# Relation messages in a phase of their own, over edges ranked by relation, stored and gathered by edge

## What is computed

```python
def rgcn_layer(x, src, dst, edge_type, W, root, bias):
    xj = x[src]
    out0 = x @ root + bias
    def body(out, inputs):
        r, Wr = inputs
        mask = (edge_type == r).astype(x.dtype)
        s = segment_sum(xj * mask[:, None], dst, num_segments=N)
        cnt = segment_sum(mask, dst, num_segments=N)
        h = s / jnp.maximum(cnt, 1.0)[:, None]
        hb = h.reshape(N, 64, 4)
        return out + jnp.einsum('nbi,bio->nbo', hb, Wr).reshape(N, d), None
x = relu(rgcn_layer(x0, ..., W1, root1, bias1))
x = rgcn_layer(x, ..., W2, root2, bias2)
x1 = layernorm(x0 + x)
```

## Time and profile before

| | us |
|---|---|
| median of 3 runs | 9330.65 (9306.11 to 9335.38) |
| span of the profiled execution | 9339.1 |
| PE, DVE, ACT, POOL busy in it | 7917.3, 7634.8, 5028.6, 4377.3 |
| l1a, first to last gather's start | 2292.6 to 3490.9 |
| l1b, the same | 3506.0 to 4969.8 |

### The profile page before, as it was taken

The page is one execution under the profiler, slowest core; times in us unless marked ns, Lnnn a source line. Parts: engine busy times, 40 slices in busy tenths (PEclk is TensorE's granted clock), DMA queues, the critical chain, the costliest instruction groups (busy, mean ns, idle before and its releaser), DMA issues. The chain is left out here.

```text
span 9339.1 us, 213338 instructions
## 1 busy us (share of the span) xinstructions
PE 7917.3 (85%) x37713; PEld 5838.0 (63%) x37714; DVE 7634.8 (82%) x29986; ACT 5028.6 (54%) x17446; POOL 4377.3 (47%) x6104
## 2 busy tenths in 40 slices
PE   7661798888888887777778999989999999989999
PEld 2220777776666665555555666666666666668887
DVE  7665577777999889999997999887777767779998
ACT  0000088887223334444444777766666656667777
POOL 3771055554777765665653333332222222245554
PEclk7555599999999998999998999997666655589999
DMA  0002233333333334444443544443444434434444
GB/s 14 2 2 32 67 112 118 115 116 111 112 113 110 104 103 126 126 125 123 126 122 113 153 146 148 146 149 113 119 122 120 124 114 121 121 113 126 127 126 120
DMA packets 1075782, 1027.30 MB, mean 110 GB/s; under 512 B 201077, under 2 KB 1029893, under 8 KB 1074974
## 3 DMA queue, kind: packets, MB, share of 16 engines
q1 hardware_dynamic: 946910, 869.10, 30.6%
q0 software_dynamic: 128576, 155.65, 7.3%
HBM read 867.45 MB, written 318.18 MB: 127 GB/s over the span
## 5 line engine op out<-in xcount | busy, mean ns | idle before, releaser
L1077 PE MATMUL l1b_ps_b<-root,l1b_x_t 128*128 128x256 f32 x1584 | 485.6, 435 | 327.3 <-DVE l1b_message L990 327.2
L188 POOL DMA_INDIRECT l_gathered<-x,l_index x402 | 473.0, 1177 | 335.2 <-POOL l_index L184 184.2
L184 POOL COPY l2b_index<-by_src_meta 128x1 int32 (+1 forms) x406 | 84.2, 207 | 1135.4 <-PE l2b_ps_g L1558 1133.7
L1077 PEld LDWEIGHTS l1b_ps_b<-root,l1b_x_t 128*128 128x128 f32 x1584 | 327.0, 216 | 459.8 <-issue 410.7
L188 POOL DMA_INDIRECT l1a_gathered<-x,l1a_index x400 | 449.2, 1123 | 333.5 <-POOL l1a_index L184 315.1
L188 POOL DMA_INDIRECT l_gathered<-in_x,l_index x402 | 441.4, 1098 | 334.3 <-POOL l_index L184 183.7
L469 POOL DMA_INDIRECT item_records<-sort_slot_rec,sort_place x400 | 476.8, 1192 | 240.4 <-issue 232.8
L188 POOL DMA_INDIRECT l1b_gathered<-h,l1b_index x400 | 428.2, 1070 | 333.0 <-POOL l1b_index L184 300.0
L188 POOL DMA_INDIRECT l2b_gathered<-z,l2b_index x406 | 420.9, 1037 | 338.4 <-POOL l2b_index L184 204.4
L188 POOL DMA_INDIRECT l2a_gathered<-x,l2a_index x402 | 411.2, 1023 | 334.1 <-POOL l2a_index L184 243.6
L1077 PE MATMUL l1a_ps_b<-root,l1a_x_t 128*128 128x256 f32 x1584 | 422.1, 389 | 156.5 <-DVE l1a_message L990 156.5
(11 more groups left out here) (365 smaller groups left out, 26999.1 us busy)
## 6 DMA issues: line engine op xcount, KB each, us to landing
l2b_x<-z SPq DMA_DIRECT2D x414, 128.0 KB, 2.1
l2a_x<-x SPq DMA_DIRECT2D x410, 128.0 KB, 2.7
l1a_x<-x SPq DMA_DIRECT2D x406, 128.0 KB, 2.7
l1b_x<-h SPq DMA_DIRECT2D x406, 128.0 KB, 2.9
l1b_res<-x SPq DMA_DIRECT2D x404, 128.0 KB, 2.6
l2b_x_again<-z SPq DMA_DIRECT2D x404, 128.0 KB, 2.4
l_x<-in_x SPq DMA_DIRECT2D x402, 128.0 KB, 2.1
l_x<-x SPq DMA_DIRECT2D x402, 128.0 KB
```

What stands on the lines that cost most here:

```text
L184: pool.tensor_copy(index[:, slot, :], graph.meta[:, bass.ds(item, 1), OTHER].bitcast(I32))\
L188: pool.indirect_dma_start(gathered[:, slot, 0:D], None, source[0:N_NODES, :], bass.IndirectOffsetOnAxis(ap=index[:, slot, :], axis=0), bou ...
L1077: pe.matmul(sums, x_t[:, k, f * P:(f + 1) * P], root[:, f, :], start=(f == 0), stop=False)
```

## The change

Each edge gets a place in a list ordered by relation, where each relation begins at a full chunk of 128: 216 chunks. The ranking is done by DVE at the head of the sort, and the place travels as a fifth word of the edge's record. During `count_edges` POOL scatters the edges' sources to their places by 200 indirect DMAs. A new phase before each relation layer gathers the source rows of each chunk, transposes them, multiplies them with the relation's block weights laid out as two wide 128x128 matrices, and stores the messages. The relation layer then gathers messages instead of rows of x. The kind rows, the block product and DVE's two message steps go, and the bias add moves from POOL to DVE.

```diff
--- before.py
+++ after.py
-K3 = 3 * GROUP
+CHUNK_RING = 8
+CHUNKS = -(-(N_EDGES // P + R1) // CHUNK_RING) * CHUNK_RING
+MESSAGES = CHUNKS * P
...
-OTHER, NODE, KIND, WEIGHT = range(4)
+OTHER, NODE, KIND, WEIGHT, MESSAGE = range(5)
+FIELDS = 5
...
-def gather_rows(pool, graph, s, index, gathered, source, extra=0, more=None):
+def gather_rows(pool, graph, s, index, gathered, source, extra=0, field=OTHER, count=N_NODES):
...
-        pool.tensor_copy(index[:, slot, :], graph.meta[:, bass.ds(item, 1), OTHER].bitcast(I32))\
+        pool.tensor_copy(index[:, slot, :], graph.meta[:, bass.ds(item, 1), field].bitcast(I32))\
...
-        pool.indirect_dma_start(gathered[:, slot, 0:D], None, source[0:N_NODES, :],
+        pool.indirect_dma_start(gathered[:, slot, 0:D], None, source[0:count, :],
...
-            if more and k % 2:
-                step(Pair(g, k // 2 + ahead))
...
+                dve.memset(going_on[:], 1.0)
+                dve.tensor_copy(relations.source[:], raw[:, 0, :])
+                chain.step(dve.tensor_tensor(in_relation[:],
+                                             rec[:, 1, :, KIND].unsqueeze(1).broadcast_to([EP, R1, EC]),
+                                             c.iota[0:EP, 0:R1].unsqueeze(2).broadcast_to([EP, R1, EC]), ALU.is_equal))
+                chain.step(dve.memset(going_on[:, :, 0:1], 0.0))
+                chain.step(dve.tensor_tensor_scan(seen[:].rearrange("p r c -> p (r c)"),
+                                                  going_on[:].rearrange("p r c -> p (r c)"),
+                                                  in_relation[:].rearrange("p r c -> p (r c)"), 0.0, ALU.mult, ALU.add))
+                dve.tensor_copy(per_row[:], seen[:, :, EC - 1]).then_inc(s_per_row, 1)
+                dve.wait_ge(s_before_row, 1)
+                chain.step(dve.tensor_scalar(chunks_i[:], ps_rel[:, R1:2 * R1], float(P - 1), None, ALU.add))
+                chain.step(dve.tensor_single_scalar(chunks_i2[:], chunks_i[:], 7, op=ALU.logical_shift_right))
...
+                chain.step(dve.tensor_tensor(seen[:], seen[:], first_place[0:EP, :].unsqueeze(2).broadcast_to([EP, R1, EC]),
+                                             ALU.add))
+                chain.step(dve.tensor_tensor(seen[:], seen[:], in_relation[:], ALU.mult))
+                chain.step(dve.tensor_reduce(message[:], seen[:].rearrange("p r c -> p c r"), AX.X, ALU.add))
...
+                dve.scalar_tensor_tensor(relations.place[:], message_lane[:], float(CHUNKS), message_chunk[:],
+                                         ALU.mult, ALU.add)
+                chain.step(dve.tensor_tensor(passed_chunks[:],
+                                             last_chunk[0:1, :].unsqueeze(1).broadcast_to([1, CHUNKS, R1]),
+                                             c.iota[0:1, 0:CHUNKS].unsqueeze(2).broadcast_to([1, CHUNKS, R1]), ALU.is_le))
+                chain.step(dve.tensor_reduce(chunk_kind[:], passed_chunks[:], AX.X, ALU.add))
+                dve.tensor_scalar(relations.kind[:], chunk_kind[:], float(R1 - 1), None, ALU.min)
...
+                pool.memset(nobody[:], FAR).then_inc(s_nobody, 1)
+                pool.wait_ge(s_padded, 16)
+                for column in range(EC):
+                    part = column // LISTS
+                    if part >= 2 and column % LISTS == 0:
+                        pool.wait_ge(s_listed[part % 2], part // 2 * LISTS * 16)
+                    pool.indirect_dma_start(rel_source[:], bass.IndirectOffsetOnAxis(ap=relations.place[:, column:column + 1],
+                                                                                     axis=0),
+                                            relations.source[:, column:column + 1], None).then_inc(s_listed[part % 2], 16)
+                for k in range(2):
+                    pool.wait_ge(s_listed[k], EC // 2 * 16)
+                    pool.sem_inc(s_sources, 1)
...
+                sp.wait_ge(s_sources, 2)
+                sp.dma_start(relations.index[:], rel_source.rearrange("(p c) o -> p (c o)", p=P)).then_inc(s_indexed, 16)
+                sp.wait_ge(s_indexed, 16)
...
+                dve.tensor_scalar(graph.first[:], graph.keep[:], -1.0, 1.0, ALU.mult, ALU.add)
...
+def message_phase(nc, c, relations, name, blocks, x_in, messages):
...
+                sp.dma_start(wide[:], blocks).then_inc(s_wide, 16)
+                rows = messages.rearrange("(c p) d -> p c d", p=P)
+                with sp.Fori(0, laps) as lap:
+                    for n in range(R // 2):
+                        sp.wait_ge(s_message, lap * (R // 2) + (n + 1))
+                        sp.sem_inc(s_passed, 1)
+                        sp.dma_start(rows[:, bass.ds(lap * R + 2 * n, 2), :], message[:, 2 * n:2 * n + 2, :])\
+                            .then_inc(s_stored[n], 16)
...
+                pool.memset(gathered[:], 0.0).then_inc(s_zeroed, 1)
+                pool.wait_ge(s_zeroed, 1)
+                for chunk in range(CHUNKS):
+                    if chunk >= R:
+                        pool.wait_ge(s_turned, (chunk - R) // 2 + 1)
+                    pool.indirect_dma_start(gathered[:, chunk % R, :], None, x_in[0:N_NODES, :],
+                                            bass.IndirectOffsetOnAxis(ap=relations.index[:, chunk:chunk + 1], axis=0),
+                                            bounds_check=limit, oob_is_err=False).then_inc(s_g[chunk % R], 16)
...
+                def turn(lap, n):
+                    for k in (2 * n, 2 * n + 1):
+                        pe.wait_ge(s_g[k], (lap + 1) * 16)
+                        for f in range(2):
+                            last = pe.transpose(ps_x[n % 2][:, k % 2, f * P:(f + 1) * P], gathered[:, k, f * P:(f + 1) * P],
+                                                c.ident[:])
+                    last.then_inc(s_turned, 1)
+
+                def product(lap, n, kinds):
+                    pe.wait_ge(s_xt, lap * (R // 2) + (n + 1))
+                    for k in (2 * n, 2 * n + 1):
+                        for f in range(2):
+                            last = pe.matmul(ps_m[n % 2][:, k % 2, f * P:(f + 1) * P], x_t[:, k, f * P:(f + 1) * P],
+                                             wide[:, f, bass.ds(kinds[k], 1), :].rearrange("p r o -> p (r o)"),
+                                             start=True, stop=True)
+                    last.then_inc(s_product, 1)
...
+                with pe.Fori(0, laps - 1) as lap:
+                    pe.load(regs, relations.kind[0:1, bass.ds(lap * R, R)])
+                    kinds = [pe.snap(r, min_val=0, max_val=R1 - 1) for r in regs]
+                    for n in range(R // 2):
+                        if n < 2:
+                            pe.wait_ge(s_message, lap * (R // 2) + n)
+                        else:
+                            pe.wait_ge(s_message, lap * (R // 2) + (n - 1))
+                        product(lap, n, kinds)
+                        turn(lap + (n + 2) // (R // 2), (n + 2) % (R // 2))
...
+                with dve.Fori(1, laps) as lap:
+                    for n in range(R // 2):
...
+                        dve.wait_ge(s_product, lap * (R // 2) + (n + 1))
+                        dve.tensor_copy(message[:, 2 * n:2 * n + 2, :], ps_m[n % 2][:]).then_inc(s_message, 1)
...
-                move_tiles(sp, graph, s, x, x_in, result, x_out, later, lead=6)
+                move_tiles(sp, graph, s, x, x_in, result, x_out, later, lead=4)
...
-                gather_rows(pool, graph, s, index, gathered, x_in, more=(add_bias, 0 if residual is None else 2))
+                gather_rows(pool, graph, s, index, gathered, messages, field=MESSAGE, count=MESSAGES)
...
+                def add_bias(pair):
+                    if residual is None:
+                        dve.wait_ge(s["total"], pair.item + 3)
+                        dve.tensor_tensor(biased[:, pair.both, :], total[:, pair.both, :], both_bias, ALU.add)\
+                            .then_inc(s["biased"], 1)
+                    else:
+                        for j, k in pair.each():
+                            pass_wait(dve, s, s["in_res"][k], (pair.lap + 1) * 16)
+                        dve.tensor_tensor(biased[:, pair.both, :], res[:, pair.both, :], both_bias, ALU.add)\
+                            .then_inc(s["res_done"], 2)
...
-                steps = [(ready, 3), (lambda p: add_up(p, 0), 1), (lambda p: multiply(p, 0), 3), (lambda p: add_up(p, 1), 1),
-                         (lambda p: multiply(p, 1), 3)]
                 if residual is None:
-                    steps += [(make_hot, 3), (add_parts, 3), (make_kind, 6)]
+                    steps = [(lambda p: add_up(p, 0), 1), (make_hot, 3), (lambda p: add_up(p, 1), 1), (add_bias, 0)]
                 else:
-                    steps += [(add_residual, 1), (make_hot, 3), (add_parts, 3), (lambda p: norm.invert(dve, p), 0),
-                              (make_kind, 6), (lambda p: norm.shift(dve, p), 0), (centre, 1)]
```

(45 more changed lines are left out.)

219 lines of the change are left out of this document (120 added, 99 removed).

## The result

| | before | changed |
|---|---|---|
| median of the runs | 9333.0 us (9306.1 to 9384.8, 4 runs) | 8975.7 us (8903.2 to 9028.6, 4 runs) |
| profiled execution, its span | 9339.1 us | 8901.4 us |

The ratio is 0.961 (0.955 to 0.967). The forecast was 9177 with 8990 as its lower end: the change gained 357 us where 154 to 156 were forecast. The changed kernel was run again later, beside variants (e5): median 9007.2 (8811.5 to 9059.4, 6 runs) beside 9325.0, 0.966 by the medians. A ratio with an interval leaves out executions more than 1.5% above the quickest of their kernel, so that of e5, 0.950 (0.945 to 0.955), rests on two of its six, 8811.5 and 8913.0. The changed kernel spreads over 2.8% there, the kernel before over 0.7%. Runs e1 to e4, e5 to e8 and e9 to e12 were made at three times, each group on a chip of its own.

What follows compares the result with a forecast made beforehand. VectorE and GpSimd were taken to bound l1a, VectorE alone l1b. Terms -286 - 523 + 638 + 36 - 19 = -154 gave 9177 us against the median; 8-in-10 range 8990 to 9410.

Steps and rivals of the forecast that it cites:

- the signs named as right: l1a gathers 2.2 to 2.3 us apart, l1b's 2.3 to 2.4; 216 gathers in about 300 us; clock 0.9 or more.
- l1a: -286 forecast: First relation layer: GpSimd the next bound, an item falling from 2.96 to 2.25 us over 402 items.
- the case that each addition catches a copy: l1a: VectorE bias adds block GpSimd's index copies, 2.39 us an item rather than 2.25, 56 us more.
- l1b: -523 forecast: Second relation layer: an item falling from 3.65 to 2.35 us over 402 items, ends 2.12 and 2.85.
- The 0.15 us that I added: l1b: allowance per item above the largest of three bounds (2.05 to 2.2), which do not hide each other wholly.
- The rival of 2.85: l1b: loop of ScalarE and VectorE does not overlap, 2.85 us an item, gain 322 instead of 523, total 9378; chance 0.12.
- Message phases: +638 forecast: Two new phases before the relation layers: 216 chunks at 1.40 us plus 17 for phase change, 319 us each.
- Ranking: +36 forecast: Head of the sort: VectorE's ranking steps take 36 us that nothing hides, since GpSimd's 400 scatters start later.
- Weights: -19 forecast: Before the count phase: VectorE's bfloat16 splitting and some transfers go, saving 19 us, ends -14 and -25.
- Listing: 0 forecast: Count phase: 200 source scatters, 298 us, hidden by VectorE and TensorE with some 14 us to spare.
- its rival: Relation layers: TensorE's clock falls, waits for ScalarE's copy being idle gaps; at 1.2 GHz for good 10038 us; chance 0.10.
- "clean" rival: GpSimd runs unhindered: 2.05 and 2.12 us an item, 1.32 a chunk, -360 us, total 8971; chance 0.16.

Runs made afterwards that it cites:

- e5: The changed kernel itself, unaltered, run again beside its variants: median 9007.2 us beside 9325.0, 0.966 by the medians.
- e1: Kernel before with 188 idle semaphore increments ahead of VectorE's l2b loop: 9118.4 us beside 9319.1, ratio 0.978.
- e4: Changed kernel with GpSimd's listing scatters held back until VectorE finished the counting half of the count phase: counting half 140.6 us; no total time given.
- e8: Changed kernel with 12 chunks in flight in the message phases instead of 8: 339.6 us a message phase; no total time given.
- e9: Kernel before with 8 idle increments ahead of VectorE's l2b loop: 9041.7 us beside 9335.0, one run.
- e12: Changed kernel with the stores of the second message phase left out: that phase 333.1 us, the first, with stores, 334.6; no total time given.
- e2: Changed kernel with 68 idle increments, putting VectorE's l2b loop where it begins in the kernel before (remainder 177 by 256): 8783.7 us.
- e3: Changed kernel with the bias additions of both relation layers back on GpSimd: 9242.5 us, one run.
- e11: The same kernel as e4, run again on e12's chip: counting half 140.7 us, count phase 449 us; no total time given.
- e10: Kernel before with 94 idle increments ahead of VectorE's l2b loop: 9179.1 us beside 9335.0, one run.

## Why the prediction was wrong, point by point

**l2b was taken as unchanged.** This is the step that failed. The sum put it at nothing; it gave 241 us in the profile. 200 of them (e1, medians) are a defect of the kernel before: its VectorE loop was fetched again every lap. The other 41 are of the size of what the stretch at clock 0.98 gave (57 items in 200 us for 44, an estimate of 60 us). The defect stood in the views I had: 282 packets of q14, and 246.3 us of "issue" before one instruction, 96 times. Against the kernel before with 188 idle instructions the change gains 335 us on that chip (e2 against e1), and 351 by the two profiles: +29 up to the count phase, +588 messages, -350 l1a, -603 l1b, -36 l2b, +19 l3, +2 elsewhere and rounding. Without the 241 us of l2b the first profile's 197 would have stood near the 154, but by luck: the two layers gained 137 more than forecast, and message phases, ranking, listing and l3 lost 94 more. Of the signs named as right, the clock came true; VectorE was 46% busy in l1a for 55, the count phase took 356 us for 318.

**l1a: -286 forecast, -346 measured.** The bound was named rightly (GpSimd; e3), the size missed: 2.25 an item for 2.11. The gather took 1.037 us and the copy 0.253, where I had carried over 1.124 and 0.340 from a kernel with a full VectorE. The prediction put 2.39 on the case that each addition catches a copy; the copy takes 0.253 us with VectorE's additions and 0.187 without (e3), 0.07 us an item and not 0.34. The rule of the Trainium skill that it quotes ("SBUF — State Buffer", "Who interferes with whom") agrees with this in kind.

**l1b: -523 forecast, -600 measured.** 2.35 for 2.16. The 0.15 us that I added because three equal bounds hide each other badly was too much: 2.16 is no more than the largest of the three as I had reckoned them (2.2). The rival of 2.85 fell. VectorE's residual addition took 425 ns (`l1b_summed`) where it took 695. GpSimd's additions alone do not explain it: with them back (e3) it takes 423.

```profile
L1172 DVE SCALAR_TENSOR_TENSOR l1b_summed<-l1b_total,l1b_biased 128x256 f32<-128x256 f32 x378 | 145.9, 423 | 356.7 <-POOL l1b_biased L1148 356.7
```

In e3 it waits for GpSimd's addition and starts behind it, so whether the two slow each other side by side stays open.

**Message phases: +638 forecast, +672 measured**, 1.497 us a chunk for 1.40, just past the upper end of 1.49; 1.305 in e2, just under the lower of 1.32. The gather is 1.00 and the gap 0.30 as reckoned; the rest is the long gaps, unexplained.

**Ranking: +36 forecast.** The first scatter moved from 133.4 to 176.0 us, +43. The compare with two broadcast inputs and the large reduction took 5.81 and 5.86 us where I had 3.8 each:

```profile
24.30 5.81 DVE L382 TENSOR_TENSOR sort_in_relation<-sort_rec,iota 125x3200 f32<-125x3200 f32 x1
...
46.25 5.86 DVE L401 TENSOR_REDUCE sort_message<-sort_seen 125x200 f32<-125x3200 f32 x1
```

**Weights: -19 forecast, -17 measured** (+26 less +43).

**Listing: 0 forecast, +36 measured.** I asked whether the list ends in time (it did: its last scatter began at 1167.9, 36 us before VectorE's last `count_hot_t`), and not what 200 scatters do to the engine beside them.

**The clock** stayed at 0.98 in both layers; its rival fell. The gap that spoke for it was there: in 500 us of l1a in e5 TensorE stood still 118 times ahead of its products with `root`, once in nearly every pair, 0.66 us each, and its clock was 0.99. 8971 us, the "clean" rival's figure, is near the result by accident: its periods (2.05, 2.12 and 1.32) were not met, and l2b made up the difference. l3's +16 does not need the change: e9 and e10, kernels before, have 1071 and 1073 us there, e1 has 1054; its cause is open.

## What to carry to other kernels

Before summing the terms of a change, look for stalls of the old kernel in code that the change does not touch but may move: a queue of instruction packets that grows with the laps of a loop, and "issue" before one and the same instruction every lap, are a place that another edit may cure by moving it, and here they were worth more than the edit's own forecast. Work put on an idle engine is free only if its neighbours do not feel it: ask of GpSimd's indirect transfers what they do to VectorE. And a wait of 0.8 us behind an index copy can be taken away by copying one pair ahead, but look first how far behind the next bound stands.

## What the runs showed that I had not expected

- One loop of 279 instructions on VectorE was fetched again each lap, five packets of 8 KB, at 200 us in 50 laps; 8, 94 or 188 idle instructions in front of it ended that. The same remainder in the changed kernel (e2) did not bring it back.
- One program (e4 and e11) has two paces of GpSimd's back-to-back gathers: phases of 294 us on one chip and 338 on another, while the kernel before has medians of 9319 to 9335 beside all runs. That its copies and waits between gathers hide the difference is argued, not shown.
- In l2b TensorE is over 90% busy and its granted clock moves between 0.60 and 0.98 within one execution; at 0.64 an item takes 4.5 us, at 0.98 3.5. The number of such stretches differs from execution to execution (l2b 1634.7 to 1847.5 us over these programs without the fetches); that it makes most of the changed kernel's spread is likely and not shown, for only one execution of each was profiled: in e5 the mean granted clock falls from 0.877 to 0.839 from the quickest to the slowest. The kernel before, held up in every lap, showed none above 0.65 in the windows from 6477 us on.
